# State rows added to y by accumulating transfers from GpSimd, with new step places, a stacked half-precision dt product and a prologue inside the main program

## The chip, the cores and the metric

One core of one Trainium2 chip runs the kernel. The metric is the device time of one execution in microseconds (us), the median of several runs. Engines are named as the profile names them: PE (TensorE) with its weight loads PEld, DVE (VectorE), ACT (ScalarE), POOL (GpSimd) and SP (SyncE), which here only issues transfers.

## What is computed

The input is 8 sequences of 1024 tokens with 256 features, all float32. Each passes a Mamba-like mixer and a mixture of experts, both modulated by a row that belongs to the sequence. Cut to what matters:

```python
mod = silu(c) @ wmod                       # per sequence: shift, 1 + scale, gate, twice
h = layernorm(x) * (1 + ca) + sa
hn = rmsnorm(h) * norm_w
xi, z = split(hn @ in_proj_w.T)            # 512 + 512 channels
u = silu(causal_conv4(xi) + conv_b)
dt, B, C = split(u @ x_proj_w.T, [16, 32]) # 16 + 16 + 16 columns
delta = softplus(dt @ dt_proj_w.T + dt_proj_b)
for t in tokens:                           # state s: 512 channels x 16
    s = s * exp(delta * A) + delta * B * u
    y = sum_n s[:, n] * C[n]
y = (y + u * D) * silu(z)
x = x + ga * (y @ out_proj_w.T + h)
h = layernorm(x) * (1 + cb) + sb
out = x + gb * (shared_mlp(h) + top-4-of-16 experts(h))
```

## The kernel before

The 8192 tokens are cut into 16 chunks of 512 (`CH`). The program runs 18 slots; in slot t three stages of three neighbouring chunks lie side by side: `prepare` of chunk t (norms, in-projection, convolution, delta), `scan` of chunk t-1, and `mix` of chunk t-2 (z, out-projection, second norm, router, experts). So slot 0 only prepares, slots 1 to 16 scan, and slot 17 only mixes.

The scan has 16 steps, one for each state index s, each over 4 channel blocks b of 128. For each block ACT computes exp(delta*A) into one of two PSUM tiles (`exp`, L839, `da_ps`), POOL multiplies delta*u by the broadcast row of B (`scaled`, L639, `db_sb`, a ring of NDB = 6 tiles), and DVE runs the recurrence over 512 tokens (`scan`, L995, `states`). A step's states are then transposed by PE into two PSUM tiles, 128 tokens (index j) at a time (`rows`, L1178, `rows_ps`), scaled by column C[s] and added to the output tile `y_sb`. For j = 0 and 2 DVE does that in one instruction (`gather`, L1014). For j = 1 and 3 ACT scales into a ring of three tiles (`c_scale`, L817, `c_rows`) and POOL adds these to `y_sb` (`c_add`, L651).

POOL also does `du` (L628), `r_gate` and `r_add` (L619, L623), `y_gate` (L659), small root computations (L596, L610, L666) and the router weight of each expert unit (`e_weigh`, L681). The experts are 36 units for each chunk: `expert_in` (L1236, 12 matmuls), `e_tanh` on ACT (L905), `e_act` and `e_mul` on DVE (L1089, L1095), `e_weigh`, and `expert_out` (L1251).

Each engine takes its instructions strictly in the order in which they were written, and waits at each for semaphores. This order comes from a planner, `schedule`: every step has a due place, a number worked out from its stage's rules and a table `SHIFT` with one number for each kind of step, and the steps of all stages are sorted by place. All engines walk the one sorted list. Three PSUM banks (`bank_ps`) are handed out along that list. Only the order in the list counts; the places are not times.

Before the slots there is a prologue in a block of its own: SP issues the 13 loads of the weights, all engines wait for all of them, the modulation rows of all sequences are computed on PE and DVE (L416, L391 to L409) and stored to memory, and the semaphores are cleared (L316) between barriers. Only then is the first chunk loaded (`x_load`, L553) and the first modulation row (`mod_p`, L503).

Delta's product `dtp` (L1160) is in float32 with 16 rows of contraction; its input comes from `xd` (L1145, 16 small matmuls), a copy on DVE (`xd_evac`, L965), a transpose (`xd_t`, L1153) and a copy on ACT (L775).

## Time and profile before

| what | value |
|---|---|
| time, median of 3 runs (lowest, highest) | 3053.87 us (3050.2, 3055.23) |
| time of the profiled execution | 3054.61 us |
| its span, from the first instruction to the last | 3052.8 us |
| DVE busy, share of the span | 84% |
| POOL busy | 84% |
| PE busy | 82% |
| ACT busy | 60% |
| share of the 16 transfer engines' time, all queues | 18.4% |

A busy time is a union over instructions, with the modelled tails of pipelined matmuls in it. Slots can be told apart in the trace by the issue of `x_load`, which comes at 1490.53, 1668.93, 1849.47, 2028.96, 2207.66 and 2387.14 us and so on.

### The profile page before, as it was taken

How to read it: one execution, taken by the hardware profiler on the slowest of the kernel's cores; microseconds unless marked ns; L12 is line 12 of the kernel's file. 1: busy time of each engine (PE TensorE's matmuls, PEld its weight loads, DVE VectorE, ACT ScalarE, POOL GpSimd, SP SyncE). 2: the span in 40 equal slices, each digit the busy share in tenths (PEclk: the TensorE clock that was granted, in tenths of full speed). 3: DMA queues.
4: the chain of work that ended last, by engine and by line, in shares of the span. 5: the costliest groups of instructions: out<-in, count | busy, mean ns of one | idle time of the engine just before them, and what ended most of it. 6: DMA issues, size and time to landing. Idle time of an engine off the chain costs nothing.

```text
span 3052.8 us, 52878 instructions
## 1 busy us (share of the span) xinstructions
PE 2488.1 (82%) x16524; PEld 1983.2 (65%) x16524; DVE 2568.1 (84%) x3986; ACT 1830.3 (60%) x3484; POOL 2563.1 (84%) x2379
## 2 busy tenths in 40 slices
PE   2566988879888797988879798887979888797979
PEld 0344766757676675767667576776757667576767
DVE  3579899888898988889898888889888898988953
ACT  2666666666666665665657566665656656665531
POOL 1689898989989898998989889898988989898942
PEclk7557998999999998999989899999989999999989
DMA  1311111211112111121112111121212211111101
GB/s 64 107 56 58 64 56 64 71 57 61 56 61 72 62 61 53 60 68 64 63 52 77 56 60 59 64 66 55 74 41 73 68 56 60 60 58 58 67 32 49
DMA packets 62150, 187.97 MB, mean 62 GB/s; under 512 B 12040, under 2 KB 14728, under 8 KB 61488
## 3 DMA queue, kind: packets, MB, share of 16 engines
q1 hardware_dynamic: 61872, 184.58, 18.0%
q8 instruction: 135, 2.21, 0.3%
q14 instruction: 143, 1.17, 0.1%
HBM read 166.68 MB, written 17.87 MB: 60 GB/s over the span
## 4 chain that ended last, share of the span: by engine, by line
POOL 29%; PE 27%; DVE 17%; issue 16%; ACT 9%; DVEq 1%; POOLq 1%; ACTq 0%; DMA 0%
POOL db_sb L639 12%; PE bank_ps L1236 9%; DVE states L995 7%; POOL y_sb L651 6%; PE moe_ps L1251 6%; PE rows_ps L1178 5%; POOL act L681 3%; POOL y_sb L659 2%; PE bank_ps L1160 2%; ACT da_ps L839 2%; DVE y_sb L1014 2%; DVE bank_ps L950 2%; DVE act L1089 1%; PE bank_ps L1134 1%; POOL du_sb L628 1%
## 5 line engine op out<-in xcount | busy, mean ns | idle before, releaser
L639 POOL TENSOR_TENSOR db_sb<-du_sb,b_sb 128x512 f32<-128x512 f32 x1024 | 1296.6, 1275 | 0.1
L1178 PE MATMUL rows_ps<-ident,states 128*128 128x128 f32 x4096 | 673.2, 295 | 163.7 <-DVE states L995 94.3
L651 POOL TENSOR_TENSOR y_sb<-y_sb,c_rows 128x512 f32<-128x512 f32 x512 | 655.1, 1280 | 169.8 <-ACT c_rows L817 169.8
L839 ACT ACTIVATE da_ps<-delta,a_sb 128x512 f32<-128x512 f32 x1024 | 701.8, 687 | 85.7 <-DVE states L995 84.2
L1178 PEld LDWEIGHTS rows_ps<-ident,states 128*128 128x128 f32 x4096 | 535.3, 153 | 281.9 <-DVE states L995 133.0
L1251 PE MATMUL moe_ps<-eout_sb,act 128*128 128x256 f32 x2304 | 627.7, 396 | 85.2 <-POOL act L681 83.5
L1236 PE MATMUL bank_ps<-h2T_high,ein_w_high 128*128 128x256 f16 x2304 | 644.0, 280 | 21.8 <-DVE delta L971 12.0
L995 DVE TENSOR_TENSOR_SCAN states<-da_ps,carry,db_sb 128x512 f32<-128x512 f32 x512 | 648.4, 1274 | 15.0 <-ACT da_ps L839 13.2
L1236 PE MATMUL bank_ps<-h2T_high,ein_w_low 128*128 128x256 f16 x2304 | 643.1, 279 | 0.0
L1236 PE MATMUL bank_ps<-h2T_low,ein_w_high 128*128 128x256 f16 x2304 | 642.4, 279 | 0.0
L995 DVE TENSOR_TENSOR_SCAN states<-da_ps,db_sb 128x512 f32<-128x512 f32 x512 | 616.2, 1213 | 23.2 <-ACT da_ps L839 13.0
L681 POOL TENSOR_TENSOR act<-act,w_sb 128x256 f32<-128x256 f32 x512 | 372.7, 729 | 165.6 <-DVE act L1095 119.6
L1251 PEld LDWEIGHTS moe_ps<-eout_sb,act 128*128 128x128 f32 x2304 | 407.5, 197 | 152.8 <-POOL act L681 108.5
L1014 DVE SCALAR_TENSOR_TENSOR y_sb<-rows_ps,xd_sb,y_sb 128x512 f32<-128x512 f32 x512 | 378.4, 739 | 106.3 <-PE rows_ps L1178 105.4
L817 ACT ACTIVATE c_rows<-rows_ps,xd_sb 128x512 f32<-128x512 f32 x512 | 349.5, 683 | 178.3 <-PE rows_ps L1178 174.8
L905 ACT ACTIVATE act<-bank_ps 128x256 f32<-128x256 f32 x576 | 219.2, 381 | 325.6 <-PE bank_ps L1236 321.5
L1089 DVE SCALAR_TENSOR_TENSOR act<-act,bank_ps 128x256 f32<-128x256 f32 x576 | 232.7, 404 | 118.3 <-ACT act L905 118.3
L1236 PEld LDWEIGHTS bank_ps<-h2T_high,ein_w_high 128*128 128x128 f16 x2304 | 230.9, 100 | 74.4 <-DVE delta L971 16.1
L1236 PEld LDWEIGHTS bank_ps<-h2T_high,ein_w_low 128*128 128x128 f16 x2304 | 230.8, 100 | 50.4 <-issue 4.6
L1095 DVE TENSOR_TENSOR act<-act,bank_ps 128x256 f32<-128x256 f32 x576 | 241.2, 419 | 17.2
L1236 PEld LDWEIGHTS bank_ps<-h2T_low,ein_w_high 128*128 128x128 f16 x2304 | 230.9, 100 | 31.7
L768 ACT ACTIVATE th_p<-bank_ps 128x512 f32<-128x512 f32 x64 | 38.2, 597 | 234.2 <-DVE bank_ps L950 234.1
(156 smaller groups left out, 2851.1 us busy)
## 6 DMA issues: line engine op xcount, KB each, us to landing
b_sb<-b_dram SPq DMA_DIRECT2D x128, 512.0 KB, 3.6
w_sb<-w_dram SPq DMA_DIRECT2D x128, 512.0 KB, 4.0
th_p<-x_dram SPq DMA_DIRECT2D x16, 512.0 KB, 5.8
r_dram<-conv SPq DMA_DIRECT2D x16, 512.0 KB, 2.6
x<-r_dram SPq DMA_DIRECT2D x16, 512.0 KB, 3.8
out_dram<-x SPq DMA_DIRECT2D x32, 256.0 KB, 2.2
mod_p<-mod_dram SPq DMA_DIRECT2D x8, 384.0 KB, 6.2
x<-e_in_dram SPq DMA_DIRECT2D x5, 512.0 KB, 4.6
```

Of the source, the lines that this page charges most:

```text
L639: pool.tensor_tensor(db_sb[:, n % NDB, :], du_sb[:, slots[t][0][0], b, :], b_sb[:, k % NBPAIR, s % BPAIR, :], ALU.mult).then_inc(sem["scal ...
L651: pool.tensor_tensor(place, place, c_rows[:, n % NCR, :], ALU.add).then_inc(sem["c_added"], 1)
L681: pool.tensor_tensor(place, place, w_sb[:, k % NWROWS, n % WROWS, :], ALU.mult).then_inc(sem["e_weighed"], 1)
L817: ac.activation(c_rows[:, n % NCR, :], rows_ps[j % 2][:, :], ACT.Copy, scale=xd_sb[:, slots[t][0][0], j, AT_C + s:AT_C + s + 1]).then_inc( ...
L839: ac.activation(da_ps[n % NDA][:, :], delta[:, slots[t][0][0], b, :], ACT.Exp, scale=a_sb[:, b, s:s + 1]).then_inc(sem["exp_done"], 1)
L995: v.tensor_tensor_scan(states[:, n % (2 * NB), :], da_ps[n % NDA][:, :], db_sb[:, n % NDB, :], first, ALU.mult, ALU.add).then_inc(sem["sca ...
L1014: v.scalar_tensor_tensor(place, rows_ps[j % 2][:, :], xd_sb[:, par, j, AT_C + s:AT_C + s + 1], place, ALU.mult, ALU.add).then_inc(sem["gat ...
L1089: v.scalar_tensor_tensor(place, place, 1.0, bank(key)[:, 0:HALF], ALU.add, ALU.mult).then_inc(sem["e_acted"], 1)
L1095: v.tensor_tensor(place, place, bank(key)[:, HALF:CH], ALU.mult).then_inc(bank_read(key)[0], 1)
L1178: last = pe.transpose(rows_ps[j % 2][:, b * P:b * P + P], states[:, step % 2 * NB + b, j * P:j * P + P], ident[:, :])
L1236: last = pe.matmul(bank(key)[:, a * HALF:a * HALF + HALF], ein_w16[w][:, k, e // 2, at:at + HID], h2T[h][:, k, q * HALF:q * HALF + HALF], ...
L1251: last = pe.matmul(moe_ps[:, n, :], act[:, u % 3, n * P:n * P + P], eout_sb[:, e, :], start=first and n == 0, stop=u % NALL == NALL - 1, s ...
```

## The change

It has four parts.

First, `gather` is gone, and all four j of a step go through ACT: `c_scale` writes pairs of rows into `c_rows`, now a ring of three pairs. POOL adds a pair to `y_sb` no more itself; it issues a transfer from SBUF to SBUF with `accum_op=ALU.add`, 512 KB, two for each step. Each is issued only when the one of the step before on the same pair has landed, and `y_gate` and the ring's reuse wait for landings too. To make room, the `db_sb` ring goes from 6 to 5 tiles and the expert weight rows are loaded in pieces of two rows instead of four (twice as many loads on SP).

Second, the places: SHIFT has new numbers, and new tables `PLACE` (for each index of a step), `FIRST`, `LAST` and `START` move single steps. Places of one kind of step can't fall behind those of the slot before.

Third, `xd` is computed with the 48 outputs on partitions (4 float32 matmuls of 512 columns in place of 16 of 48), and `dtp` takes 80 rows of float16: the high half of dt, its low half and the high half again, against the high half of the weight twice and its low half. ACT makes the high half twice (`dt_high`), DVE the low one (`dt_low`), and the transpose for C is no more ahead of `dtp`.

Fourth, the prologue's block and its barriers are gone. The loads are issued in another order, with x of the first chunk as the fourth; the first sequence's modulation is computed straight onto 128 partitions (`mod0`), and the other rows later; each consumer waits for what it needs.

```diff
-NDA, NDB, NCR = 2, 6, 3
-C_ACT = (1, 3)
+NDA, NDB, NCR = 2, 5, 3
+CPAIR = 2
...
-WROWS, NWROWS = 4, 2
+WROWS, NWROWS = 2, 2
...
-            out += [(at + 0.145, ("c_scale", t, s, j)), (at + 0.892, ("c_add", t, s, j))] if j in C_ACT else [(at + 0.156, ("gather", t, s, j))]
+            out.append((at + 0.145, ("c_scale", t, s, j)))
+            if j % CPAIR == CPAIR - 1:
+                out.append((at + 0.892, ("c_add", t, s, j // CPAIR)))
...
+            at = round(at + SLOT * t + SHIFT.get(what[0], 0.0) + PLACE.get(place(what), 0.0) + ends.get(what[0], 0.0), 5)
+            latest[what[0]] = max(at, latest.get(what[0], at))
+            out.append((latest[what[0]], t, n, what))
...
-        with nc.Block() as block:
-            @block.sync
-            def _(sp):
-                for dst, src in LOADS:
-                    sp.dma_start(dst, src).then_inc(sem["weights_in"], 16)
...
-        clear_semaphores()
...
+                    def first_loads():
+                        sp.dma_start(ct_sb, c_t).then_inc(sem["ct_in"], 16)
+                        sp.dma_start(wmod_sb[:, :, 0:3 * DM], w_mod[:, :, 0:3 * DM]).then_inc(sem["wmod_in0"], 16)
+                        sp.dma_start(norm_sb[:, :], norm_w).then_inc(sem["in_w_in"], 16)
+                        x_load(0)
+                        sp.dma_start(in_raw, in_w).then_inc(sem["in_w_in"], 16)
...
-                        pool.wait_ge(sem["c_added"], max(0, n - len(C_ACT) + 1))
+                        if step:
+                            pool.wait_ge(*c_adds(n - NJ // CPAIR))
                         if s == 0 and t > 0 and slots[t - 1][1] is not None:
                             pool.wait_ge(*bank_read(("skip_t", t - 1, NB - 1)))
-                        place = y_sb[:, slots[t][0][0], j, :]
-                        pool.tensor_tensor(place, place, c_rows[:, n % NCR, :], ALU.add).then_inc(sem["c_added"], 1)
+                        pool.dma_start(y_sb[:, slots[t][0][0], CPAIR * pair:CPAIR * pair + CPAIR, :], c_rows[:, n % NCR, :, :],
+                                       accum_op=ALU.add).then_inc(c_adds(n)[0], 16)
...
+                    def dt_high(t):
+
+                        if t == 0:
+                            ac.wait_ge(sem["dt_zeroed"], 2)
+                        if nP(t):
+                            ac.wait_ge(*bank_full(("dtp", last_prepare(t), NB - 1)))
+                        ac.wait_ge(*bank_full(("xd", t)))
+                        for at in (DT_HIGH, DT_AGAIN):
+                            ac.activation(dt16[at:at + RANK, :], bank(("xd", t))[0:RANK, :], ACT.Copy).then_inc(sem["dt_high_done"], 1)
...
-                        ac.wait_ge(sem["c_added"], max(0, n - NCR + 1))
-                        ac.activation(c_rows[:, n % NCR, :], rows_ps[j % 2][:, :], ACT.Copy,
-                                      scale=xd_sb[:, slots[t][0][0], j, AT_C + s:AT_C + s + 1]).then_inc(sem["c_scaled"], 1)
+                        if n >= NCR:
+                            ac.wait_ge(*c_adds(n - NCR))
+                        ac.activation(c_rows[:, n % NCR, j % CPAIR, :], rows_ps[j % 2][:, :], ACT.Copy,
+                                      scale=xd_sb[:, slots[t][0][0], j, s:s + 1]).then_inc(sem["c_scaled"], 1)
...
-                    def gather(t, s, j):
...
-                        pe.matmul(bank(key), dtw_sb[:, b * P:b * P + P], xdT[0:RANK, :], start=True, stop=True).then_inc(bank_full(key)[0], 1)
+                        pe.matmul(bank(key), dtw16[:, b * P:b * P + P], dt16[:, :], start=True, stop=True).then_inc(bank_full(key)[0], 1)
```

What the change does to the order is seen best on three pieces. On POOL, late in the scan of a middle chunk, stood before (db_sb rows are `scaled`, y_sb rows `c_add`, act rows `e_weigh`):

```order
L639 TENSOR_TENSOR db_sb<-du_sb,b_sb 128x512
L651 TENSOR_TENSOR y_sb<-y_sb,c_rows 128x512
L639 TENSOR_TENSOR db_sb<-du_sb,b_sb 128x512
L681 TENSOR_TENSOR act<-act,w_sb 128x256
L651 TENSOR_TENSOR y_sb<-y_sb,c_rows 128x512
L639 TENSOR_TENSOR db_sb<-du_sb,b_sb 128x512
```

At the same place of the changed program stands on POOL:

```order
L681 DMA y_sb<-c_rows 128x1024
L669 TENSOR_TENSOR db_sb<-du_sb,b_sb 128x512
L712 TENSOR_TENSOR act<-act,w_sb 128x256
L681 DMA y_sb<-c_rows 128x1024
L712 TENSOR_TENSOR act<-act,w_sb 128x256
L669 TENSOR_TENSOR db_sb<-du_sb,b_sb 128x512 x2
```

Two additions of 512 columns in each step have become two issued transfers of 1024 columns, and the products for the scan stand as close around them as before.

On ACT, at the same place, stood before (da_ps rows are `exp`, c_rows rows `c_scale`, act rows `e_tanh`):

```order
L839 ACTIVATE da_ps0<-delta,a_sb 128x512
L817 ACTIVATE c_rows<-rows_ps1,xd_sb 128x512
L839 ACTIVATE da_ps1<-delta,a_sb 128x512
L905 ACTIVATE act<-bank_ps1 128x256
L817 ACTIVATE c_rows<-rows_ps1,xd_sb 128x512
L839 ACTIVATE da_ps0<-delta,a_sb 128x512
L905 ACTIVATE act<-bank_ps2 128x256
L839 ACTIVATE da_ps1<-delta,a_sb 128x512
```

And now:

```order
L886 ACTIVATE c_rows<-rows_ps0,xd_sb 128x512
L979 ACTIVATE act<-bank_ps1 128x256
L913 ACTIVATE da_ps0<-delta,a_sb 128x512
L886 ACTIVATE c_rows<-rows_ps1,xd_sb 128x512
L913 ACTIVATE da_ps1<-delta,a_sb 128x512
L886 ACTIVATE c_rows<-rows_ps0,xd_sb 128x512
L886 ACTIVATE c_rows<-rows_ps1,xd_sb 128x512
L913 ACTIVATE da_ps0<-delta,a_sb 128x512
```

ACT now also empties `rows_ps0`, so four `c_scale` stand in each step between its four `exp`.

On SP, the program began before with all weights, and the first chunk (th_p<-x_dram) came after the barriers, whose rows are the branch and the 16 ISA instructions:

```order
L341 DMA y_sb<-w_mod_dram 128x3072
L341 DMA th_p<-c_t_dram 128x16
L346 DMA mod_dram<-db_sb 8x512 x3
L337 UNCONDITIONAL_BRANCH
L316 ISA x16
L494 UNCONDITIONAL_BRANCH
L503 DMA mod_p<-mod_dram 128x768
L553 DMA th_p<-x_dram 128x1024
```

Now it begins with:

```order
L488 UNCONDITIONAL_BRANCH
L491 DMA states<-c_t_dram 128x16
L492 DMA y_sb<-w_mod_dram 128x2x768
L493 DMA norm_sb<-norm_w_dram 128x2
L564 DMA th_p<-x_dram 128x1024
L495 DMA states<-in_w_dram 128x2048
```

The first chunk's load has moved ahead of the large weights, and nothing of the modulation's way through memory stands ahead of it.

## Rows read from the trace of the kernel before

**Rows 1.** Page, busy time of each engine.

```profile
PE 2488.1 (82%) x16524; PEld 1983.2 (65%) x16524; DVE 2568.1 (84%) x3986; ACT 1830.3 (60%) x3484; POOL 2563.1 (84%) x2379
```

**Rows 2.** Busy time by slot (2 to 17; two middle ones), and the last stretch.

```profile
core 0: us, PE busy (x) PEld busy (x) DVE busy (x) ACT busy (x) POOL busy (x), PEclk, DMA share, GB/s
2028.96:2207.66 178.70, 150.52 (x1034) 120.95 (x1032) 159.70 (x248) 113.15 (x214) 159.56 (x149) 0.95 0.19 64
2207.66:2387.14 179.48, 153.25 (x1034) 122.99 (x1032) 156.78 (x248) 113.53 (x220) 159.59 (x149) 0.93 0.18 60
2920.00:3052.80 132.80, 110.69 (x754) 89.75 (x751) 55.79 (x129) 27.92 (x61) 37.64 (x49) 0.94 0.13 43
```

**Rows 3.** Groups of instructions over these two slots, 2028.96 to 2387.14 us.

```profile
L639 POOL TENSOR_TENSOR db_sb<-du_sb,b_sb 128x512 f32<-128x512 f32 x129 | 163.1, 1272 | 0.0
L651 POOL TENSOR_TENSOR y_sb<-y_sb,c_rows 128x512 f32<-128x512 f32 x64 | 81.4, 1271 | 21.3 <-ACT c_rows L817 21.3
L1014 DVE SCALAR_TENSOR_TENSOR y_sb<-rows_ps,xd_sb,y_sb 128x512 f32<-128x512 f32 x65 | 48.0, 739 | 12.8 <-PE rows_ps L1178 12.8
L817 ACT ACTIVATE c_rows<-rows_ps,xd_sb 128x512 f32<-128x512 f32 x64 | 43.7, 683 | 19.6 <-PE rows_ps L1178 19.3
L619 POOL TENSOR_TENSOR conv<-u_sb,mod_p 128x1024 f32<-128x1024 f32 x2 | 4.7, 2349 | 0.0
L596 POOL TENSOR_TENSOR rstd<-rstd,minus_half 128x4 f32<-128x4 f32 x2 | 2.1, 1038 | 0.2
```

**Rows 4.** Waits in the same two slots.

```profile
POOL y_sb L651 <- ACT c_rows L817: 21.3, 12, 6.1
POOL act L681 <- DVE act L1095: 6.5, 6, 1.7
POOL act L681 <- DMA w_sb<-w_dram: 6.2, 2, 3.2
POOL du_sb L628 <- DVE delta L971: 3.0, 2, 1.5
```

**Rows 5.** The scans' and the dt product's instructions, whole span.

```profile
L995 DVE TENSOR_TENSOR_SCAN states<-da_ps,db_sb x512: 1190/1215/1225, 112.6 to 2764.4; 128x512 f32<-128x512 f32 x171
L995 DVE TENSOR_TENSOR_SCAN states<-da_ps,carry,db_sb x512: 1254/1275/1284, 264.7 to 2925.3; 128x512 f32<-128x512 f32 x171
L1160 PE MATMUL bank_ps<-th_p,dtw_sb 16*128 16x512 f32 x128 | 78.2, 698 | 0.8 <-ACT th_p L775 0.8
L1134 PE MATMUL bank_ps<-hnT_low,in_w_high 128*128 128x512 f16 x128 | 52.7, 412 | 0.0
```

**Rows 6.** Transfers: time of the queue's packets, and issue to landing (us).

```profile
q1 hardware_dynamic: 61872, 184.58, 18.0%
b_sb<-b_dram SPq DMA_DIRECT2D x128, 512.0 KB, 3.6
th_p<-x_dram SPq DMA_DIRECT2D x16, 512.0 KB, 5.8
r_dram<-conv SPq DMA_DIRECT2D x16, 512.0 KB, 2.6
```

**Rows 7.** Timeline of the prologue and of the first chunk.

```profile
12.92 0.17 DVE L369 TENSOR_SCALAR th_p<-th_p 128x16 f32<-128x16 f32 x1 [12.92 <-DMA th_p<-c_t_dram]
13.62 5.10 PE L416 MATMUL bank_ps<-y_sb,th_p 128*8 128x512 f32 x8 [13.62 <-DVE th_p L372]
30.54 0.43 SPq L553 DMA_DIRECT2D th_p<-x_dram  x1
35.22 0.43 DVE L924 BATCH_NORM_STATS2 bn<-th_p 128x6 f32<-128x256 f32 x1 [9.93 <-DMA th_p<-x_dram]
39.60 1.55 ACT L700 ACTIVATE bank_ps<-th_p,rstd 128x256 f32<-128x256 f32 x3 [26.32 <-POOL rstd L602]
40.69 0.70 DVE L933 TENSOR_TENSOR bank_ps<-bank_ps,mod_p 128x512 f32<-128x512 f32 x1 [3.24 <-ACT bank_ps L700]
85.64 7.19 PE L1160 MATMUL bank_ps<-th_p,dtw_sb 16*128 16x512 f32 x8 [0.76 <-ACT th_p L775]
```

More of the change, by code:

```diff
@@ L41 @@
 AT_B, AT_C = RANK, RANK + NS
+DT_HIGH, DT_LOW, DT_AGAIN, DTK = 0, 32, 64, 64 + RANK
 LIFT = 64.0
 NPAIR = NE // 2 + 1
[L47 to L49 removed]
+NDA, NDB, NCR = 2, 5, 3
+CPAIR = 2
 NBANK = 3
@@ new lines, with place, start_steps @@
+START = {"constants": 0.018, "ct_tanh": -1.588, "first_loads": 5.582, "fold": 1.987, "in_high": -3.563, "in_low": 0.718, "mod0": 0.251,
+         "mod_rows": -0.032, "mod_store": -0.045, "mods": 1.704, "out_scale": -2.535}
+def place(what):
+    return "_".join(str(n) for n in (what[0], *(what[3:] if what[0] in ("exp", "scaled", "scan", "rows", "c_scale", "c_add") else what[2:])))
+def start_steps():
+    out = [(-9, ("first_loads",)), (-9, ("constants",)), (-8, ("ct_tanh",)), (-8, ("ct_silu",)), (-7, ("mod0",)), (6.2, ("mod0_rows",)), (9.0, ("mod0_gate",))]
+    out += [(-6, ("norm_lift",))] + [(6.3, ("in_high", k)) for k in range(NK)] + [(7.6 + 3.0 * k, ("in_low", k)) for k in range(NK)]
+    out += [(7.7, ("fold",)), (10.7, ("mods",)), (18.5, ("mod_rows",)), (18.5, ("mod_store",)), (18.5, ("a_made",)), (12.0, ("out_scale",))]
+    return out
@@ L428, in rows_in, with run_slots @@
+        def run_slots(slots, load_mod_p, load_mod_m):
+            order, places = schedule(slots, load_mod_p, load_mod_m)
             def rows_in(load_mod, t):
```

423 lines of the change are left out of this document (255 added, 168 removed), and 52 rows, old and new, of the table PLACE.

## The prediction

> **What bounds the kernel now.** I read the page's busy times first. Three engines stand close together, DVE and POOL at 84% and PE at 82%, and ACT is far behind at 60% [rows 1]. So no single engine fills the span, and the share alone does not say which one to relieve. The table by slot says more. In two middle slots of 178.70 and 179.48 us (mean 179.1) POOL is busy 159.6 us in each, always the same to 0.03 us, DVE 159.7 and 156.8 (mean 158.2), PE 150.5 and 153.3 (mean 151.9), ACT 113.3 [rows 2]. There are 16 slots with a scan, and almost the whole time lies in them, so what the change is worth is what it takes from one such slot.
>
> The third view is the groups over these two slots. POOL's product for the scan, 64 for each slot, waits for nothing (0.0 us idle before 129 of them) [rows 3]. So POOL comes to that product late and always finds it ready: whenever POOL reaches its next scan product, DVE has long freed the tile. POOL is the engine that paces the slot, with DVE 1.4 us behind. POOL's idle time is 179.1 - 159.6 = 19.5 us, and the waits name nearly all of it: half of 21.3, 6.5, 6.2 and 3.0 us, thus 18.5 us for each slot, of which 10.7 us is the addition to y_sb waiting for ACT's scaled rows [rows 4]. Taking work from POOL and DVE together is what can shorten the slot, as long as PE at 151.9 us doesn't take over at once.
>
> **Part one, the state rows.** From DVE go 32 `gather` instructions in each slot, 32 x 0.739 = 23.6 us [rows 3]. DVE comes to 158.2 - 23.6 = 134.6 us, and some small copies of 16 rows don't change that. ACT gets as many `c_scale`: 32 x 0.683 = 21.9 us [rows 3], and two small copies for dt, at most 0.7 us each by the same row. ACT comes to 113.3 + 21.9 + 1.4 = 136.6 us. That is 76% of today's slot and 84% of the one I forecast, so ACT loses its ease but is not the bound. From POOL go 32 additions, 32 x 1.271 = 40.7 us [rows 3], which leaves 118.9 us. To it come 32 issued transfers at a price c each.
>
> Nothing in this trace issues a transfer from POOL, so c has to be bounded. Below: SP issues the 512 KB load of x in 0.43 us [rows 7]. It hands its work to hardware, so POOL is unlikely to do it in less. Above: the 128x1024 instruction with which POOL would itself work through as many elements takes 2.35 us [rows 3]. Between them lies what POOL needs for an instruction with next to no data but a program of its own, 1.04 us for 128x4 elements [rows 3]. The issue is of that kind, since it computes addresses for 128 rows and touches no data. I take c = 1.0, and POOL's slot becomes 118.9 + 32 = 150.9 us.
>
> The Trainium skill ("DMA: Bandwidth & Descriptors", section "Latency and other measured facts") gives about 1 us to the first byte of a transfer issued from GpSimd, for the emission of its descriptors; no run here shows it yet, and by it the sum would be the same 150.9 us.
>
> What is queued behind the new waits: `c_add` stands on POOL ahead of the next scan products. It waits for ACT's second row of the pair, as the old addition did, and for the landing of the same pair's transfer one step earlier. A step is 179.1 / 16 = 11.2 us. A 512 KB transfer lands 2.6 to 5.8 us after its issue [rows 6]; doubled for the second read it is 5.2 to 11.6 us. I take 7 us, inside the step, and cost this wait at nothing. If the cover goes, DVE is late next, because POOL's products no longer come (second rival). For the engines that carry the transfers: 184.58 MB took 18.0% of 3052.8 us, 549 us, or 0.336 MB per us [rows 6]. The additions move 512 x 0.524 = 268 MB, which is 799 us at that rate and 1598 us if the second read doubles it, 50 to 100 us in each slot beside today's 33. That fits into 163 us. The ring of 5 in place of 6 products costs nothing, because the scan products never waited for it; the doubled number of smaller loads is 16 more issues of under 0.45 us for each slot on SP, which is otherwise waiting.
>
> **Part three, the dt product.** Four float32 products are 78.2 / 16 = 4.9 us of PE in a slot, four float16 ones of the same columns at most 4 x 0.41 = 1.6 us [rows 5]. That saves 3.3 us of PE busy time, so PE comes to 148.6 us. `xd` changes from many small to four large float32 matmuls and I count it even. With POOL at 150.9 none of this is on the path that sets the slot; it matters for the bound behind it.
>
> **Part two, the places.** They are worth what they do to idle time. Today POOL idles 19.5 us in a slot. Three of the four causes stay in place, but the largest, the wait for ACT's rows, hangs on DVE's scans, and DVE gains 23 us of room, while ACT gets fuller. I keep about 60%, 12 us, with 5 and 19.5 as ends. The slot is then 150.9 + 12 = 163 us, 16.1 less than now. There are 15 such slots. The first scanning slot has no experts; its scans run from 112.6 to 264.7 us [rows 5], and there I take off only what POOL saves plus a little, 10 us. Together 15 x 16.1 + 10 = 251 us.
>
> **Part four, the prologue.** Now the first chunk's load is issued at 30.54 us, its statistics start at 35.22 and the modulation is multiplied on at 40.69 [rows 7]. After the change it is the fourth issue, at some 2 us, and lands by 8. The other input to that multiply is the first modulation row: c_t and half of w_mod landed, then one and a half of the three products that take 5.1 us for two of them [rows 7]. All loads were there by 12.92 [rows 7]; a fourth of their bytes by 8. So the products run from about 9 to 13 and the multiply starts near 15.5, 25 us earlier. From there the chain is the same one up to the first scan at 112.6 us, only that the four dt products took 7.19 us there [rows 7] and now take about 7.19 x 1.6 / 4.9 = 2.4; two more copies ahead of them give half of it back. I take 27 us in all. The ends are 15 (if the remaining loads and the second half of the weight split are late for the in-projection) and 32.
>
> **The end.** After the last scan at 2925.3 us the last chunk only mixes, and PE is busy 110.7 of 132.8 us [rows 2]. Nothing of it changes but that the last additions must land, 5 us in place of 1.3; I add 2 us with what the new places may give.
>
> **The sum** is made against the profiled execution's own 3054.6 us, which is 0.02% above the median shown: 3054.6 - 251 - 27 + 2 = 2779, predicted 2780 us, 9% less.
>
> **The rivals.**
>
> *The issue is cheap and PE becomes the bound.* If c is 0.43 us, POOL falls to 132.7 us, DVE and ACT are at 135 and 137, and PE at 148.6 us is the highest. For it speaks only that SP's issue is that short. PE's idle time would shrink to some 8 us, because it waits mainly for the others. A slot of 157 us gives 3054.6 - 15 x 22 - 15 - 27 + 2 = 2685 us. The clock helps here: it is 0.93 to 0.95 in the slots [rows 2], so little is to be had from it.
>
> *The issue is dear.* At c = 1.5 POOL is at 118.9 + 48 = 166.9 us and the slot at 179, and only the prologue's gain is left: 3030 us. At 1.3 the slot is 172.5 and the time 2925 us. The break-even point against before lies at a slot of 180.8 us, c = 1.56. At c = 2.0 the slot would be 195 us and the time 3054.6 + 15 x 16 + 10 - 25 = 3280 us. For it speaks that the transfer has 128 rows and a second read, and that POOL's program is slow in all its rows.
>
> *The landing takes longer than the step.* This one ends on the slower side whatever the issue costs. Each pair's addition waits on POOL for the step before. Once landing and issue together exceed 11.3 us, every step lasts that long, and the scan products behind it come late. At 12 + 1 = 13 us the slot is 208 us and the time 3054.6 + 15 x 29 + 29 - 25 = 3490 us. For it: two such transfers are in flight with loads beside them, and an addition in the transfer engine is nothing that the trace shows. Against it: 3.6 us for plain loads [rows 6] leaves a factor of three.
>
> The Trainium skill ("DMA: Bandwidth & Descriptors", section "Anatomy of one DMA — SWDGE (gpsimd) path") fits 2.0 us plus the bytes at 436 GB/s, an estimate of 3.2 us for 512 KB and 4.4 us with the data read twice; no row here shows an accumulating transfer, and by it this rival would not occur.
>
> *The fuller ACT and the new order eat the gain.* ACT is in order and now has `c_scale` between the exponentials for which DVE waits with only two tiles. If idle time grew from 19.5 to 28 us at c = 1.0, the slot would be 179 and the time 3030 us. It counts with the dear issue as a small gain.
>
> **Chances.** The forecast's case, a slot between 155 and 173 us, 0.60. Cheap issue with PE bound, 0.12. Small gain of 0.2% to 4%, by a dear issue or by idle time, 0.12. Within 0.2%, about what a measurement of this kernel can tell from no change, 0.02. Slower: landing 0.09, issue above 1.56 us 0.05. That makes faster 0.84, same 0.02, slower 0.14. The range goes from 2670 us, the cheap issue, to 2940 us, c at 1.3 with a little more idle time; it holds the forecast's case, most of the cheap one and a part of the small gain.
>
> **What would show it.** In the changed kernel's trace: POOL's issue rows with c (right if 0.8 to 1.2 us); POOL and PE both near 150 us of a slot of about 163; DVE near 135, ACT near 137; no wait of POOL for the landing of additions; landing rows under 9 us; the first scan at 84 to 88 us instead of 112.6; dt products near 0.4 us each. It is wrong if POOL's idle time ahead of `c_add` is put down to the transfers, if the scans wait for `db_sb`, or if the slots are short but POOL is idle a fifth of the time, which would mean that PE or ACT is the new pace.

## The result, and the profile after

The changed kernel takes 2979.64 us (median of 4 runs, 2978.24 to 2980.74) against 3052.82 us for the kernel before: ratio 0.976, interval 0.9743 to 0.9777. It is 2.4% faster. The forecast was 2780 us with a range from 2670 to 2940 us, so the sign was right and the size three to four times too large.

The page of the changed kernel first: busy times, the two queues of transfers, and the chain that ended last by engine.

```profile
PE 2431.5 (82%) x16084; PEld 1908.7 (64%) x16084; DVE 2277.2 (76%) x3495; ACT 2129.4 (71%) x4033; POOL 2397.0 (80%) x2382
q0 software_dynamic: 73728, 268.47, 48.2%
q1 hardware_dynamic: 80560, 184.20, 19.9%
POOL 21%; issue 20%; PE 18%; DVE 15%; ACT 14%; DMA 6%; DVEq 1%; POOLq 0%; ACTq 0%; SPq 0%
```

Against [rows 1] DVE loses 291 us of work and POOL 166, ACT gains 299. No engine is above 82% now: work went away, and the time did not follow. Next, nine slots at a stroke, from one load of x to the ninth after it: before, then changed (columns as in [rows 2]).

```profile
953.50:2565.80 1612.30, 1365.10 (x9290) 1095.57 (x9289) 1427.21 (x2224) 1019.82 (x1950) 1436.18 (x1333) 0.94 0.19 62
```

```profile
924.20:2506.40 1582.20, 1338.18 (x9038) 1058.48 (x9037) 1260.26 (x1945) 1186.29 (x2254) 1343.68 (x1334) 0.95 0.71 159
```

A slot went from 1612.3 / 9 = 179.1 us to 1582.2 / 9 = 175.8, by 3.3 us where 16.1 had been forecast. In it POOL is busy 149.3 us (forecast 150.9), DVE 140.0 (134.6), ACT 131.8 (136.6), PE 148.7 (148.6). Most of the work was costed right, DVE's 5.4 us too low; POOL's idle time is 26.5 us where 12 had been forecast. The rows of POOL's three large groups in two of these slots, 1978.40 to 2329.91 us, and POOL's waits over the whole span, show where it idles:

```profile
L669 POOL TENSOR_TENSOR db_sb<-du_sb,b_sb 128x512 f32<-128x512 f32 x128 | 195.3, 1687 | 10.1 <-DVE states L1150 9.9 <-issue 0.2
L681 POOL DMA_DIRECT2D y_sb<-c_rows x65 | 77.3, 1196 | 16.3 <-DMA y_sb<-c_rows 9.2 <-ACT c_rows L886 5.8 <-issue 1.1
L712 POOL TENSOR_TENSOR act<-act,w_sb 128x256 f32<-128x256 f32 x65 | 73.4, 1181 | 21.1 <-DMA w_sb<-w_dram 14.3 <-DVE act L1237 6.7
```

```profile
POOL act L712 <- DMA w_sb<-w_dram: 119.4, 52, 22.0
POOL act L712 <- DVE act L1237: 104.5, 105, 5.8
POOL db_sb L669 <- DVE states L1150: 79.8, 22, 5.0
POOL y_sb L681 <- DMA y_sb<-c_rows: 77.1, 27, 4.8
POOL y_sb L681 <- ACT c_rows L886: 58.7, 60, 3.2
```

The wait for ACT's rows is a third of what it was (169.8 us over the span of before). In its place stand three others: for the weight rows (46.0 us before), for a free product tile (none before), and for the landing of the additions. DVE has a new wait too, for the chunk's own x. SP issues its loads in order, and in the changed kernel the load of x stands right behind one of weight rows for which SP first waits until POOL has used up a tile:

```profile
DVE bn L1068 <- DMA th_p<-x_dram: 46.6, 14, 4.0
SPq L554 <- POOL act L712: 955.1, 164, 10.2
1449.63 0.32 SPq L557 DMA_DIRECT2D w_sb<-w_dram  x1
1450.04 0.40 SPq L564 DMA_DIRECT2D th_p<-x_dram  x1
```

Before, DVE waited 11.6 us for x, nearly all of it in the prologue; issue to landing of x took 5.8 us and now takes 8.2.

In the groups above, a product that follows an issue is recorded as overlapping it (mean 1687 ns in place of 1272 in [rows 3]), so these busy times do not add up to POOL's; the table by slot does not count them twice. Two rows of the timeline show it, the second starting 0.61 us after the first:

```profile
2042.28 0.89 POOL L681 DMA_DIRECT2D y_sb<-c_rows  x1
2042.89 1.58 POOL L669 TENSOR_TENSOR db_sb<-du_sb,b_sb 128x512 f32<-128x512 f32 x1
```

The last rows of the changed kernel: the scans, the issue, the dt product, and two transfers with issue to landing.

```profile
L1150 DVE TENSOR_TENSOR_SCAN states<-da_ps,db_sb x512: 1189/1215/1226, 85.4 to 2687.1; 128x512 f32<-128x512 f32 x171
L1150 DVE TENSOR_TENSOR_SCAN states<-da_ps,carry,db_sb x512: 1255/1276/1286, 240.6 to 2852.8; 128x512 f32<-128x512 f32 x171
L681 POOL DMA_DIRECT2D y_sb<-c_rows x512: 845/907/2974, 99.3 to 2861.2; - x171
DMA to landing us min/median/max: 4.5/5.5/11.4
L1328 PE MATMUL bank_ps<-dt,dtw 80*128 80x512 f16 x4 | 1.5, 382 | 0.0
```

```profile
y_sb<-c_rows POOLq DMA_DIRECT2D x512, 512.0 KB, 5.5
w_sb<-w_dram SPq DMA_DIRECT2D x256, 256.0 KB, 4.4
```

The first scan starts at 85.4 us instead of 112.6 [rows 5], 27.2 us earlier. The first scan with a carry comes at 240.6 instead of 264.7, 24.1 us earlier, so the first scanning slot gave 3 us back where 10 more had been forecast. The last scan comes 72.5 us earlier (2852.8 against 2925.3), which is 48.4 / 15 = 3.2 us for each slot between, and what follows it is 1.9 us shorter. Together that is 74.4 us, the difference of the two profiled executions (3054.6 and 2980.2). The median issue takes 0.91 us, the median landing 5.5 us. The mean of the issues, 1.20 us, holds overlap with their neighbours; what an issue adds to POOL's busy time is read from `e2_no_adds` below, 0.88 us.

### The profile page after: what moved, and what is told of

It reads as the page before. It is cut to its first block, busy times and chain, and to the rows that moved or that the text cites. A ratio compares the mean times of both kernels' runs of the same rounds, so it can differ in the third digit from the quotient of the medians.

```text
span 2978.4 us, 52216 instructions
## 1 busy us (share of the span) xinstructions
PE 2431.5 (82%) x16084; PEld 1908.7 (64%) x16084; DVE 2277.2 (76%) x3495; ACT 2129.4 (71%) x4033; POOL 2397.0 (80%) x2382
## 3 DMA queue, kind: packets, MB, share of 16 engines
q0 software_dynamic: 73728, 268.47, 48.2%
q1 hardware_dynamic: 80560, 184.20, 19.9%
## 4 chain that ended last, share of the span: by engine, by line
POOL 21%; issue 20%; PE 18%; DVE 15%; ACT 14%; DMA 6%; DVEq 1%; POOLq 0%; ACTq 0%; SPq 0%
POOL db_sb L669 10%; PE bank_ps L1413 8%; DVE states L1150 5%; PE moe_ps L1431 4%; POOL y_sb L681 3%; POOL act L712 3%; DMA y_sb<-c_rows 3%; DMA th_p<-x_dram 3%; ACT c_rows L886 3%; ACT da_ps L913 3%; PE rows_ps L1349 2%; DVE bank_ps L1097 2%; POOL y_sb L690 2%; DVE act L1231 2%; DVE act L1237 1%
## 5 line engine op out<-in xcount | busy, mean ns | idle before, releaser
L669 POOL TENSOR_TENSOR db_sb<-du_sb,b_sb 128x512 f32<-128x512 f32 x1024 | 1575.2, 1710 | 80.3 <-DVE states L1150 79.8
L886 ACT ACTIVATE c_rows<-rows_ps,xd_sb 128x512 f32<-128x512 f32 x1024 | 684.8, 684 | 186.4 <-PE rows_ps L1349 93.9
L1349 PE MATMUL rows_ps<-ident,states 128*128 128x128 f32 x4096 | 646.8, 291 | 177.6 <-ACT c_rows L886 104.9
L712 POOL TENSOR_TENSOR act<-act,w_sb 128x256 f32<-128x256 f32 x512 | 580.8, 1185 | 224.7 <-DMA w_sb<-w_dram 119.4
L681 POOL DMA_DIRECT2D y_sb<-c_rows x512 | 608.2, 1195 | 149.9 <-DMA y_sb<-c_rows 77.1
L1349 PEld LDWEIGHTS rows_ps<-ident,states 128*128 128x128 f32 x4096 | 512.6, 150 | 273.8 <-DVE states L1150 123.6
L1097 DVE SCALAR_TENSOR_TENSOR bank_ps<-xi_pad,convw_sb,bank_ps 128x512 f32<-128x512 f32 x192 | 142.9, 744 | 24.6 <-ACT bank_ps L814 16.7
L656 POOL TENSOR_TENSOR du_sb<-delta,u_sb 128x512 f32<-128x512 f32 x64 | 94.8, 1483 | 69.1 <-DVE delta L1124 69.1
```

The source lines that it names most:

```text
L669: pool.tensor_tensor(db_sb[:, n % NDB, :], du_sb[:, slots[t][0][0], b, :], b_sb[:, k % NBPAIR, s % BPAIR, :], ALU.mult).then_inc(sem["scal ...
L681: pool.dma_start(y_sb[:, slots[t][0][0], CPAIR * pair:CPAIR * pair + CPAIR, :], c_rows[:, n % NCR, :, :], accum_op=ALU.add).then_inc(c_add ...
L712: pool.tensor_tensor(place, place, w_sb[:, k % NWROWS, n % WROWS, :], ALU.mult).then_inc(sem["e_weighed"], 1)
L886: ac.activation(c_rows[:, n % NCR, j % CPAIR, :], rows_ps[j % 2][:, :], ACT.Copy, scale=xd_sb[:, slots[t][0][0], j, s:s + 1]).then_inc(sem ...
L1349: last = pe.transpose(rows_ps[j % 2][:, b * P:b * P + P], states[:, step % 2 * NB + b, j * P:j * P + P], ident[:, :])
```

## The experiments

All times are medians; the kernel before took 3053 to 3055 us beside each set. "Slot" is the time between two loads of x, averaged over nine of them (eight where it says so).

**First set: what do the transfers cost?**

`e1_rows_on_engines` (ratio 0.9848, 0.9829 to 0.9868) undoes part one in the changed kernel:

```diff
-            out.append((at + 0.145, ("c_scale", t, s, j)))
-            if j % CPAIR == CPAIR - 1:
-                out.append((at + 0.892, ("c_add", t, s, j // CPAIR)))
+            out += [(at + 0.145, ("c_scale", t, s, j)), (at + 0.892, ("c_add", t, s, j))] if j in C_ACT else [(at + 0.156, ("gather", t, s, j))]
...
```

> The changed kernel with part one undone: the gather is again on VectorE for two of the four rows and the plain addition on GpSimd for the other two; the new places, the float16 dt product, the new prologue, the ring of 5 products and the smaller weight loads all stay. It shows what part one is worth inside the new order. Before to changed is 73 us, and the trace gives 27 of it to the prologue, so 46 us (3 us a slot) are left for the rest. Theory A (part one brings the whole rest): about 3025 us. Theory B (the new places bring part of it, and the transfers give back with waits what they save): between 2940 and 3005 us. If it is under 2970 us, the transfers cost more than they bring.

3008.9 us (2999.9 to 3016.1, the widest spread of all runs), slot 178.6: just past theory B's upper end. It looked as if part one were worth 29 us. The third set shows that this was read too early.

`e2_no_adds` (0.904, 0.9027 to 0.9052) takes the transfers and every wait on them away:

```diff
-                        pool.dma_start(y_sb[...], c_rows[:, n % NCR, :, :], accum_op=ALU.add).then_inc(c_adds(n)[0], 16)
...
```

> Leaves out the sum over the states: the transfers that add ACT's rows to y_sb aren't issued, and nobody waits for them; all products, scans and c_scale stay. GpSimd loses 32 issues of about 0.9 us in each slot, 29 us of busy time, and the transfer engines lose the heaviest load. It bounds from below what any cheaper form of the addition could reach. If the 26 us of GpSimd's idle time in a slot come from the transfers (their waits and the lateness of other loads beside them), they vanish and TensorE at 150 us sets a slot of about 158: 2979 - 15 x 17 = 2720 us. If they come from the order and from a fuller ACT, the slot stays near 170: about 2890 us or more.

2760.6 us, slot 162.8. With POOL relieved of every addition, at 121.0 us of work a slot (so an issue had cost (149.3 - 121.0) / 32 = 0.88 us of it), the slot is just what the forecast had promised with POOL at 150.9. That is nearer to the first figure, 2720, than to 2890. Its chain by engine has little of POOL left:

```profile
PE 37%; ACT 22%; DVE 15%; issue 13%; POOL 5%; DMA 2%; DVEq 1%; ACTq 0%; SPq 0%; POOLq 0%
```

`e3_small_adds` (0.9415, 0.9402 to 0.9428) keeps the issues and shrinks what they move:

```diff
-                        pool.dma_start(y_sb[:, slots[t][0][0], CPAIR * pair:CPAIR * pair + CPAIR, :], c_rows[:, n % NCR, :, :],
+                        pool.dma_start(y_sb[:, slots[t][0][0], CPAIR * pair, 0:64], c_rows[:, n % NCR, 0, 0:64],
```

> The same 512 adding transfers with the same waits, but each moves 64 columns of one row for each partition (32 KB in place of 512 KB), so that most of the sum over the states is left out. The issues and the order stay, the load on the transfer engines and the landing shrink. Theory of the load and landing: GpSimd's idle time falls by 9 us of landing waits and some of the 14/2 us for the weight rows in each slot, 12 us: 2979 - 15 x 12 = 2800 us. Theory of the issue's price or of the order: under 3 us a slot, 2935 us or more.

2874.2 us, slot 169.6 (eight slots), between the two figures. Its rows: the issue costs the same for a sixteenth of the bytes, and the waits for landings (y_sb) and for weight rows (w_sb) go from 77.1 and 119.4 to 8.7 and 50.4 us.

```profile
L681 POOL DMA_DIRECT2D y_sb<-c_rows x512: 847/942/3049, 100.4 to 2755.3; - x171
DMA to landing us min/median/max: 2.1/2.7/8.1
POOL act L712 <- DMA w_sb<-w_dram: 50.4, 18, 21.8
POOL y_sb L681 <- DMA y_sb<-c_rows: 8.7, 7, 1.6
```

DVE's wait for x is nearly gone too, 6.9 us in place of 46.6. So the bytes of the additions, by their landing and by what they delay, cost 175.8 - 169.6 = 6.2 us a slot. What is left of them, their issues with the short landings and all waits on them, costs 169.6 - 162.8 = 6.8 us, for 28 us of POOL's time.

`e4_no_row_loads` (0.9556, 0.9543 to 0.9569):

```diff
+                        if k >= NWROWS:
+                            return
                         sp.wait_ge(sem["w_stored"], 16 * (nM(t) + 1))
...
```

> Leaves out the loads of the experts' weight rows after the first two; later chunks and experts reuse those two tiles, so e_weigh never waits for such a load and 254 of 256 loads are gone. If the wait for these rows (14.3 us of two slots, 119 us in all on GpSimd) costs its full length, the time falls by 119 us to about 2860 us. If the wait only moves to the next cause (act, db_sb), it stays at 2950 us or more.

2919.1 us, 60 us less, half of the wait's length, and between the two figures. Late loads are a real cost. It is not the rows alone: SP has no tile to wait for any more, and DVE's wait for x is gone too (1.4 us).

**Second set: which part can be mended?**

`f1_ring_six` (0.9804, 0.9788 to 0.982):

```diff
-NDA, NDB, NCR = 2, 5, 3
+NDA, NDB, NCR = 2, 6, 3
...
-        wT = sb("wT", [NE, CH])[:, :]
+        wT = dt_both[96:96 + NE, :].bitcast(F32)
...
```

> The changed kernel with a ring of 6 scan products instead of 5 (wT lies in free partitions of the tile that now holds dt16 and dtw16, which makes the space). Nothing else differs. In the changed kernel GpSimd waits 79.8 us in all for scans to free a product, against 9.2 us before. If the smaller ring is a cause of the lost idle time, most of it comes back: 2979 - 60 = about 2920 us. If the wait only stands in for what the scans themselves wait for, the time stays within 0.5% of 2979 us.

2993.5 us. POOL's wait for a product tile halves, from 79.8 to 40.4 us, and the time grows by 14. The wait only stood in for others: that for the weight rows goes from 119.4 to 136.9 us, and those for the additions grow too. (The 9.2 us of before in the expectation are the opposite wait, DVE's for POOL's product. POOL had waited for no tile at all.)

`f2_single_loads` (0.9785, 0.9771 to 0.98):

```diff
-WROWS, NWROWS = 2, 2
+WROWS, NWROWS = 1, 4
```

> The changed kernel with the experts' weight rows loaded one by one into a ring of 4 instead of two by two into a ring of 2: the same space and bytes, 32 more loads issued in each pair of slots, but a place is free, and its load starts, one e_weigh earlier. Leaving out the loads altogether brought 60 us. If what they cost is that a load starts late, this gives at least half of it back: 2950 us or less. If what they cost is the load on the transfer engines beside the additions, nothing changes or the smaller transfers cost more: 2975 to 3010 us.

2987.8 us. The wait for weight rows grew to 152.3 us. Each load is still placed one step of its own ahead, now half as far. DVE's wait for x is gone here (1.5 us) and the time is no shorter, so a timely x alone does not pay while the rows come later.

`f3_old_places` (0.9814, 0.9799 to 0.9829) gives every slot after the first the shifts and slot length of before:

```diff
...
+            own = SHIFT.get(what[0], 0.0) + PLACE.get(place(what), 0.0) + ends.get(what[0], 0.0) if t == 0 else OLD_SHIFT.get(what[0], 0.0)
...
```

> The changed kernel with the places of before for every slot after the first (shift by kind of step only, no places for each index; the slot length and lead of before), the new prologue kept. It shows what the search of places brought to this form of the kernel. The prediction gave the new places 7.5 us of idle time for each slot together with the freer DVE; if that is right, this kernel takes about 2979 + 15 x 7 = 3085 us. If the places are worth little, under 3000 us.

2996.4 us, slot 177.1. The new places bring this form 17 us in all, 1.3 us a slot. The prediction had counted 7.5 us a slot for them together with DVE's new room.

`f4_quarter_on_dve` (0.9888, 0.9873 to 0.9903):

```diff
+def on_dve(s, j):
+    return s % 2 == 1 and j >= CPAIR
...
```

> The changed kernel with rows 2 and 3 of every second step gathered by VectorE as before: in each slot GpSimd issues 24 transfers in place of 32 (7 us less), the transfer engines carry a quarter less of the additions, ScalarE has 16 c_scale less (11 us less), VectorE 16 gathers more (12 us more, 152 in place of 140 us). If the transfers' load, their issues and ScalarE's fullness hold the slot at 176 us, it falls to 170 to 173 us: 2890 to 2940 us. If VectorE's own load and its waits decide, it is no better than 2980 us.

3019.1 us. The mixture adds a wait of its own. DVE's gather stands behind the landing of the pair's transfer of the step before, and POOL stands behind DVE's scans:

```profile
POOL db_sb L682 <- DVE states L1166: 210.9, 99, 4.5
DVE y_sb L1181 <- DMA y_sb<-c_rows: 142.7, 49, 5.7
```

**Third set: the cure for late rows, ScalarE, larger transfers, and the square.**

`g1_three_tiles` (0.958, 0.9558 to 0.9601):

```diff
-WROWS, NWROWS = 2, 2
+WROWS, NWROWS = 2, 3
...
-                out.append((... at - WROWS * TICK + 0.6, ("w_load", t, g)))
+                out.append((... at - (NWROWS - 1) * WROWS * TICK + 0.6, ("w_load", t, g)))
...
```

> The changed kernel with three tiles of two weight rows in place of two (the space comes from wT, as in the ring of six), and each load placed four ticks ahead of its first use in place of two. Nothing else differs. GpSimd waits 119 us for these rows in the changed kernel, and leaving out their loads brought 60 us; loading them one by one brought nothing. If the loads start too late, the third tile brings 40 to 60 us: about 2930 us. If it is their share of the busy transfer engines, the time stays within 20 us of 2980 us.

2925.8 us, the fastest kernel that computes everything. Its nine slots, and what is left of the wait:

```profile
906.70:2459.60 1552.90, 1336.95 (x9044) 1056.66 (x9042) 1259.53 (x1945) 1184.62 (x2256) 1345.11 (x1335) 0.95 0.73 162
POOL act L713 <- DMA w_sb<-w_dram: 81.0, 16, 22.0
DVE bn L1069 <- DMA th_p<-x_dram: 1.4, 1, 1.4
```

The work is the same and the engines' share of transfers too (0.73); 16 waits are left of 52, and the slot is 172.5 us. The rows had come late because they were asked for late: with two tiles a load can only start when POOL has used up the tile before, and beside the additions it then takes 4.4 us to land. Two waits went together, though. SP, held up less (734.3 us in place of 955.1), issues the load of x earlier as well, and DVE no longer waits for it. How much of the 54 us is the rows and how much is x was not separated; `f2_single_loads` shows only that x in time brings nothing while the rows come later still.

`g2_short_c_scale` (0.965, 0.9632 to 0.9668):

```diff
-                        ac.activation(c_rows[:, n % NCR, j % CPAIR, :], rows_ps[j % 2][:, :], ACT.Copy,
+                        ac.activation(c_rows[:, n % NCR, j % CPAIR, 0:64], rows_ps[j % 2][:, 0:64], ACT.Copy,
...
```

> Leaves out most of the sum over the states in another way: c_scale copies only 64 of 512 columns of each row, the transfers stay whole and add zeros for the rest. ScalarE loses 64 x some 0.4 us in each slot, 26 us of 132; everything else stays. (A memset of c_rows on GpSimd at the start adds a few us there.) If ScalarE's new fullness delays the exponentials and e_tanh for which VectorE waits 367 us in all, the slot falls by 5 us or more: 2900 us or less. If ScalarE has ease enough and the rest sets the pace, 2960 us or more.

```profile
914.60:2481.50 1566.90, 1333.33 (x9038) 1058.98 (x9037) 1257.02 (x1945) 986.03 (x2254) 1341.98 (x1334) 0.95 0.72 160
```

2948.9 us, between the two figures: ACT works (1186.29 - 986.03) / 9 = 22 us less in a slot, and the slot gives 1.7 us. ACT's fullness counts, but little.

`g3_fours` (1.0689, 1.0672 to 1.0706):

```diff
-NDA, NDB, NCR = 2, 5, 3
-CPAIR = 2
+NDA, NDB, NCR = 2, 5, 2
+CPAIR = 4
...
```

> The changed kernel with one transfer for all four rows of a step (1 MB, ring of 2) in place of two of 512 KB (ring of 3); the space comes from wT and from the router's temporaries, which lie in zg. Same bytes, half the issues: GpSimd loses 16 issues of 0.9 us in each slot, 14 us of busy time. From the kernels without transfers and with small ones the 32 issues are worth 7.2 us of a slot, so half of them 3.6 us: 2979 - 15 x 3.6 = 2925 us, if an issue costs the same for twice the rows. If its time doubles with them, or if the landing of 1 MB gets longer than the 11 us step, 2980 us or more.

3266.2 us. The issue is as cheap as before (median 0.88 us), the landing is not:

```profile
POOL y_sb L682 <- DMA y_sb<-c_rows: 304.0, 92, 9.2
L682 POOL DMA_DIRECT2D y_sb<-c_rows x256 | 226.0, 883 | 409.4 <-DMA y_sb<-c_rows 304.0
y_sb<-c_rows POOLq DMA_DIRECT2D x256, 1024.0 KB, 8.3
DMA 29%; PE 18%; issue 17%; DVE 13%; POOL 9%; ACT 8%; DVEq 0%; POOLq 0%; ACTq 0%
```

One issue for a step must wait for the step's last row, the step after it waits for that landing, and ACT waits 177.8 us for landings that free a place in the ring of two. The landings now make 29% of the chain. That is near the prediction's rival of the long landing, but not that rival as it was put: landing and issue together are 9.2 us at the median, below its 11.3 us, and only the longest landing (13.3 us) is above. The router's temporaries also moved into `zg` here, and what that costs was not separated.

`g4_engines_old_places` (0.9714, 0.9698 to 0.973) is the first experiment with the edit of `f3_old_places`.

> The first experiment (rows on the engines) with the old places for every slot after the first: what is left of the change is the new prologue, the float16 dt product, the ring of 5 and the smaller weight loads. It completes the square of rows (engines, transfers) and places (old, new): transfers with old places 2996, with new ones 2980, engines with new places 3009 us. If the prologue is worth its 27 us and the rest nothing, this is 3053 - 27 = 3026 us; then the places brought 17 us to either form and the transfers 30 us with either places. Over 3035 us, the ring and the smaller loads cost something; under 3018 us, the dt product brought something.

2967.5 us, where 3026 had been expected. With the rows on the engines and the old places the kernel is 12 us faster than the changed one. Its nine slots:

```profile
912.30:2495.50 1583.20, 1334.46 (x9038) 1064.50 (x9037) 1427.88 (x2233) 1027.92 (x1968) 1436.11 (x1333) 0.95 0.20 63
```

DVE and POOL carry the old 158.7 and 159.6 us, and the slot is 175.9 us, the same as the changed kernel's. The square is: engines 2967 (old places) and 3009 (new), transfers 2996 and 2980. The new places fit the transfers and harm the other form by 41 us, which is why the first experiment misled. With either set of places held fixed, the transfers cost 29 us (old) or bring 29 (new).

**Fourth set: whose microseconds count?**

`h1_dt_thrice_engines` (0.9787, 0.977 to 0.9803) and `h2_dt_thrice_transfers` (0.9846, 0.9831 to 0.9861) make the dt product three times, in the kernel of 2967 us and in the changed one:

```diff
...
+                        for n in range(3):
+                            last = pe.matmul(bank(key), dtw16[:, b * P:b * P + P], dt16[:, :], start=True, stop=True)
+                        last.then_inc(bank_full(key)[0], 1)
```

> The kernel of 2967 us (rows on the engines, old places, new prologue), with each of the four dt products of a slot made three times into the same bank, so that the float16 product costs TensorE about what the float32 one did: 8 x 0.41 = 3.3 us more for each slot. If these microseconds are on the path that sets the slot, all or most of the 60 us go again: 2967 + 16 x 3.3 = 3020 us. If GpSimd paces this form, as the prediction read it, the time stays within 10 us of 2967, and the 60 us come from something else.

> The changed kernel with the same three-fold dt products, 3.3 us more of TensorE for each slot. If TensorE's chain sets the slot in this form too, 2979 + 53 = 3032 us. If the transfers' waits and ScalarE's set it, and TensorE has ease, under 3000 us.

2989.1 and 3008.8 us, so 22 and 29 us, between the figures both times. Three products in a row do not take PE three times as long; the group's rows without and with them, and one such triple, show it:

```profile
L1349 PE MATMUL bank_ps<-dt,dtw 80*128 80x512 f16 x64 | 24.9, 393 | 1.0 <-DVE dt L1120 0.5 <-ACT delta L856 0.5
L1350 PE MATMUL bank_ps<-dt,dtw 80*128 80x512 f16 x192 | 54.9, 399 | 0.6 <-DVE dt L1120 0.6
1033.87 0.81 PE L1350 MATMUL bank_ps<-dt,dtw 80*128 80x512 f16 x3
```

The edit adds 54.9 - 24.9 = 30 us of PE, not the float32 product's 78.2 - 24.9 = 53 that the expectation had wanted to put back. Of these 30 us, 22 count in the engines' form (0.7) and 29 in the transfers' (nearly all), though POOL and DVE are 10 us a slot busier than PE in the first. About 3.5 us of each lie ahead of the first scan, which comes at 89.9 instead of 86.4 us and at 89.2 instead of 85.4. The slot itself grows by 0.7 and 1.6 us.

`h3_small_extra_engines` (1.0183, 1.0167 to 1.0198):

```diff
...
+                        pool.tensor_scalar(tiny_sb[:, n % 64, :], minus_half[:, :], 1.0, None, ALU.mult).then_inc(sem["spared"], 1)
...
```

> The kernel of 2967 us with one more instruction of GpSimd on 128x4 elements behind each product for the scan, into a tile of its own that nobody reads: 64 x 0.235 = 15 us more busy time for each slot, which takes GpSimd from 159.5 to 174.5 of today's 176 us. If GpSimd paces the slot with 16 us of idle time that cannot be removed, the slot grows by 15 us: 2967 + 16 x 15 = 3207 us. If it has slack that the others' pace leaves it, the slot grows by a quarter to a half of it, as in the kernels without additions (29 us of issues were worth 7): 3030 to 3090 us.

```profile
953.60:2613.10 1659.50, 1344.19 (x9038) 1064.94 (x9037) 1437.38 (x2233) 1028.33 (x1968) 1547.54 (x1909) 0.94 0.19 60
```

3110.7 us. POOL's work grew by (1547.54 - 1436.11) / 9 = 12.4 us a slot and the slot by 184.4 - 175.9 = 8.5 us: 0.69 us for each. POOL sets most of the pace in the engines' form, but not all.

`h4_engines_old_rings` (0.9689, 0.9673 to 0.9704):

```diff
-NDA, NDB, NCR = 2, 5, 3
+NDA, NDB, NCR = 2, 6, 3
...
-WROWS, NWROWS = 2, 2
+WROWS, NWROWS = 4, 2
```

> The kernel of 2967 us with the ring of 6 products and two tiles of four weight rows, as before the change. What is left of the change is then the prologue and the float16 dt product alone. If the ring of 5 and the smaller loads cost nothing, as the prediction has it, within 8 us of 2967 us. If one of them costs something, 2930 to 2955 us, and this is the best form so far beside the one with three tiles.

2959.7 us, 8 us less: just within what had been called no cost, but the runs of the two kernels don't overlap (2955.7 to 2964.4 against 2967.0 to 2970.4). What remains of the change here is the prologue, the new dt and xd steps and their places, and it is worth 95 us.

`h5_engines_three_tiles` (0.9718, 0.9705 to 0.9732) and `h6_transfers_old_places_three_tiles` (0.9772, 0.9759 to 0.9785) have the edit of `g1_three_tiles`:

> The kernel of 2967 us (rows on the engines, old places) with three tiles of two weight rows, loads four ticks ahead. GpSimd waits only 30 us for these rows here, against 119 in the changed kernel. If the wait counts by its length, 2967 - 25 = about 2943 us; if the old rings' 8 us were all there was, 2955 to 2967 us.

> The kernel of 2996 us (rows by transfers, old places) with the same three tiles. If late weight rows are what takes back the relief of GpSimd, it gains as much as with the new places, 50 us, and comes out level with or under the engines' form: 2945 us or less. If the additions' own landing and ScalarE's fullness take it back, it gains no more than its wait of 45 us times a half, and stays behind the engines' form: 2970 us or more.

2968.7 and 2982.3 us. The third tile brings nothing to the engines, 14 us to the transfers with old places, and 54 us with the new ones. With old places POOL waits only 44.9 us for rows, with the new ones 119.4: the places of the changed kernel had made most of the rows late. The 14 us are less than half of the wait of 44.9 us, the second figure of the last expectation, so with old places late rows are not what takes POOL's relief back; nor did that wait shrink (81.4 us, 22.2 of it in one piece), and what the 14 us are is not shown. With the third tile, transfers and new places together are 42 us faster than the engines' form of 2967 us and 34 faster than the one of 2960.

## Why the prediction was wrong

**The sum of work held.** POOL's 150.9 us (149.3), PE's 148.6 (148.7), the issue at c = 1.0 (0.88 to 0.91), the landing at 7 us (5.5), the prologue's 27 us (27.2) and the dt product's 3.3 us ((78.2 - 24.4) / 16 = 3.4) were right. DVE's 134.6 us became 140.0: by the table of nine slots its work fell by 18.6 us, from 158.6, and not by 23.6; the new copies for dt are under 1 us of the difference. POOL and PE are fuller, and the forecast did not hang on DVE. The additions took 48.2% of 2978.4 us, 1436 us, inside the bounds of 799 and 1598.

**The step that failed** is "the slot is then 150.9 + 12 = 163 us": that the slot is POOL's work plus a little, since POOL's product never waits. The 16.1 us a slot that it promised were 8.7 us of POOL's work and 7.5 us of its idle time; 3.3 came. It held three errors.

*POOL's microseconds were counted whole.* In the engines' form one counts 0.69 (`h3_small_extra_engines`). The relief is (1436.11 - 1343.68) / 9 = 10.3 us a slot, so worth some 7 us, an estimate that takes a slope measured by adding work for one by removing it. `e3_small_adds`, which has the relief and almost none of the bytes, agrees: 175.9 - 169.6 = 6.3 us against the engines' form, of which the new places, worth 177.1 - 175.8 = 1.3 us to the transfers, may be a part. DVE's relief of 18.6 us and ACT's added work are in these 6.3 us too. Further down it counts less: 6.8 us of slot for the last 28 us of issues, with PE on 37% of the chain. A group without idle time in front of it said only that POOL comes late, not that nobody else would.

*The additions' bytes were costed at nothing.* "I take 7 us, inside the step, and cost this wait at nothing" looked at one transfer and one wait. They cost 6.2 us a slot. Late loads behind them, of weight rows and of x, are at most about half of it, since the third tile brings 3.3 us; with small additions a part of the wait for rows is left (50.4 of 119.4 us), so that not all of the 3.3 us need be the bytes'. The rest I put down to the landing waits of POOL and ACT; that part was not isolated, and the slopes are read off single points. So relief and bytes nearly cancel: 175.8 us with the transfers, 175.9 us without, each with the places that suit it better.

*The places and DVE's room were to take 7.5 us of idle time.* The new places bring 1.3 us a slot to the transfers and cost the engines' form 2.7 (178.6 against 175.9). POOL's idle time did not fall from 19.5 to 12 us but rose to 26.5: the wait for ACT's rows shrank as forecast, and the waits for loads, landings and tiles took its place.

**"None of this is on the path"** failed too, for PE's 3.3 us. Putting a little over half of the cost back takes 22 us of the gain away in one form and 29 in the other. The whole 3.2 us by which the slot is shorter than before is there in `g4_engines_old_places` without any transfer.

**Where the 73 us come from**, then: prologue 27, read from the trace (no run puts the old one back); the float16 dt product 22 measured, some 38 by estimate if the rest of its 53 us counts like the first 30, and 3.5 us of either already in the prologue's 27; the rings and smaller loads minus 8; the transfers with their places minus 12. That leaves some 30 to 50 us. In the nine slots of `g4_engines_old_places` the shorter slot shows as POOL's wait for ACT's rows, 63.8 us where it had been 95.3, which says where and not why. The kernels in question differ from before also by xd as four wide products instead of sixteen narrow ones, by the order of the steps around dt, and by the work's order after the last scan, where it is worth no more than 2 us (125.8 us from there to the end, against 127.5). Which of them brings it was not tried, and it stays open.

**The rivals.** The cheap issue with PE as bound did not come, though PE's time counts. The dear issue is excluded at 0.91 us. The landing longer than the step did not come at 512 KB; at 1 MB the landings bound the chain though their median stayed below the step. The fuller ACT was right in kind, an idle time of 26.5 us where it had said 28, but it is 1.7 us of it; the transfers, which the prediction named under "what would show it", are the larger part. The result lies in the case that had been given 0.12, the small gain of 0.2% to 4% by idle time.

## What to carry to other kernels

Where four engines lie between 63% and 89% of a stage, ask of each what a microsecond is worth before costing a change: add a small dummy operation and read the slope. Here it was 0.69 on the busiest engine and 0.7 on one 11 us below it. Read from the trace what the dummy really added, since three matmuls in a row took twice the time of one and not three times. Work moved into transfers is paid again by every load that has to land beside them, so look at how far ahead each small load is asked for, and what else waits behind it in the same queue; one more tile and an earlier place were worth more than the whole move. And places chosen for one form don't price another: an edit should be undone with either set, as the square of four kernels shows.

## What the runs showed of the hardware that was not expected

The issue of an adding transfer from POOL cost about the same for each of three sizes: median 942 ns for 32 KB, 907 ns for 512 KB and 876 ns for 1 MB. The landing grew with the size: 2.7, 5.5 and 8.3 us. For each MB, adding transfers took 1436 / 268.47 = 5.3 us of the sixteen engines' time, plain ones beside them 593 / 184.20 = 3.2, and 3.0 before [rows 6]. The loads beside them landed later too: 5.1 us in place of 3.6 for the 512 KB of B's rows, 8.2 in place of 5.8 for x. The weight rows' 256 KB took 4.4 us, and 4.3 in the kernel with three tiles, so the third tile did not make them faster, only earlier. Of three float16 products of 512 columns in a row on PE, each after the first took 0.22 us more (0.81 us for three, 0.38 for one), at a granted clock of 1.00 in that stretch (1028 to 1042 us).
